# A four-layer sequence kernel: the convolution reads its input time-major from a second host layout, and the length mask moves to the dense stage

## What is computed

```python
# L0: per channel a causal convolution with a kernel of 1024 steps, masked by each sample's length
mask = arange(1024) < length[:, None]
u = x * mask[:, None, :]
x = x + (irfft(rfft(u, 2048) * rfft(kernel, 2048))[..., :1024] + u * D[:, None]) * mask[:, None, :]
# L1: per sample one of 16 channel mixes
x = x + einsum('bct,bcd->bdt', x, weights[condition])
# L2: dense 1024 x 1024 over time, bias, and one of 32 rank-16 adapters per sample
x = x + x @ W2.T + bias + (x @ A2[adapter].T) @ B2[adapter].T
# L3: dense 1024 x 1024, and one of 5 rank-32 adapters per sample
x = x + x @ W3.T + 0.5 * (x @ A3[labeler]) @ B3.T
```

## Time and profile before

| | us |
|---|---|
| median of 3 runs | 1579.5 (1578.61 to 1580.14) |
| span of the profiled execution | 1580.4 |
| convolution, 205.9 to 641.3 | 435.4 |
| dense stage from its first product, 663.6 to the end | 916.8 |
| TensorE busy | 1529.8 (97% of the span) |
| VectorE busy | 1002.2 (63%) |
| ScalarE busy | 612.5 (39%) |
| GpSimd busy | 389.7 (25%) |

### The profile page before, as it was taken

The page is one execution under the profiler, slowest core; times in us unless marked ns, Lnnn a source line. Parts: engine busy times, 40 slices in busy tenths (PEclk is TensorE's granted clock), DMA queues, the critical chain, the costliest instruction groups (busy, mean ns, idle before and its releaser), DMA issues.

```text
span 1580.4 us, 33596 instructions
## 1 busy us (share of the span) xinstructions
PE 1529.8 (97%) x11213; PEld 1477.5 (93%) x11213; DVE 1002.2 (63%) x2010; ACT 612.5 (39%) x1185; POOL 389.7 (25%) x389
## 2 busy tenths in 40 slices
PE   6899989999999999699999999999999999999998
PEld 5778879999999999599999999999999999999998
DVE  7955357888888888445556555565564555655554
ACT  3331245555555554234334343343343433434332
POOL 3551246666666666100000000000000000000000
PEclk9999999999999999699999999999999999999999
DMA  9723166666666674433533535435344353353542
GB/s 243 111 104 98 41 217 236 240 236 238 237 235 238 237 246 165 141 109 99 166 113 117 150 106 145 134 102 158 113 138 141 94 164 115 116 153 104 147 132 74
DMA packets 165111, 243.13 MB, mean 154 GB/s; under 512 B 62113, under 2 KB 118701, under 8 KB 162417
## 3 DMA queue, kind: packets, MB, share of 16 engines
q1 hardware_dynamic: 154844, 208.11, 43.7%
q10 hardware_dynamic: 10230, 34.52, 6.1%
HBM read 167.62 MB, written 74.95 MB: 153 GB/s over the span
## 4 chain that ended last, share of the span: by engine, by line
PE 58%; issue 0%; ACT 0%; DVE 0%; DMA 0%; DVEq 0%
PE ps L1538 23%; PE ps L1539 22%; PE ps L1509 7%; PE ps L1548 2%; PE ps L1546 2%; PE ps L1520 1%; PE ps L1515 0%; DMA x_in<-x_d 0%; ACT a L1310 0%; DVE weights L1406 0%; ACT xa L1312 0%; ACT weights L1322 0%; DVE y_out L1487 0%; ACT xs L1327 0%; DVE y_out L1490 0%
## 5 line engine op out<-in xcount | busy, mean ns | idle before, releaser
L1538 PE MATMUL ps<-weights,xs 128*128 128x256 f32 x1536 | 398.4, 289 | 0.0
L1539 PE MATMUL ps<-weights,xs 128*128 128x256 f32 (+1 forms) x1536 | 389.9, 293 | 0.0
L1538 PE MATMUL ps<-weights,xa 128*128 128x352 f32 (+1 forms) x1152 | 331.1, 314 | 4.4 <-DVE weights L1406 1.3
L1539 PE MATMUL ps<-weights,xa 128*128 128x256 f32 (+1 forms) x1152 | 325.9, 298 | 0.0
L1538 PEld LDWEIGHTS ps<-weights,xs 128*128 128x128 f32 x1536 | 293.2, 191 | 0.0
L1539 PEld LDWEIGHTS ps<-weights,xs 128*128 128x128 f32 x1536 | 292.4, 190 | 0.0
L1284 POOL COPY m_gath<-mix 64x64 f32 x128 | 37.6, 294 | 840.8 <-PE ps L1509 733.9
L1110 PE MATMUL ps<-toep,ut 128*128 128x512 f32 (+2 forms) x1152 | 228.8, 344 | 0.0
L1538 PEld LDWEIGHTS ps<-weights,xa 128*128 128x128 f32 x1152 | 219.1, 190 | 9.7 <-issue 9.7
L1539 PEld LDWEIGHTS ps<-weights,xa 128*128 128x128 f32 x1152 | 218.9, 190 | 0.0
L1310 ACT ACTIVATE a<-ps 128x512 f32<-128x512 f32 x128 | 76.6, 598 | 358.1 <-PE ps L1509 358.1
(11 more groups left out here) (227 smaller groups left out, 2483.5 us busy)
## 6 DMA issues: line engine op xcount, KB each, us to landing
toep_raw<-kern_d SPq DMA_DIRECT2D x64, 512.0 KB, 3.4
xt<-in_x SPq DMA_DIRECT2D x64, 512.0 KB, 4.0
x_d<-xt SPq DMA_DIRECT2D x64, 512.0 KB, 2.9
x_in<-x_d SPq DMA_DIRECT2D x64, 512.0 KB, 5.0
out<-y_out ACTq DMA_DIRECT2D x64, 512.0 KB, 4.4
stack<-b_d SPq DMA_DIRECT2D x130, 128.0 KB, 3.4
tab<-a_d SPq DMA_DIRECT2D x126, 128.0 KB, 2.1
stack<-b_d SPq DMA_DIRECT2D x128, 64.0 KB, 4.2
```

The lines of the kernel that those rows point to most:

```text
L1538: mm(left[0], x_part, left[1], start=first and is_wide, stop=end, skip_group_check=True)
L1539: ins = mm(right[0], x_part, right[1], start=first and is_wide and H_AT[m] > 0, stop=end, skip_group_check=True)
```

## The change

- The host hands over a second copy of x, `in_xt`, with axes (channel, step within a block of 128, block, sample). The convolution loads its operand from it, steps on the partitions (`xt[u][p, block, sample]`, 512 KB, four buffers, up to 3 ahead). `transpose_x` and `utf` go; `ut`, `udiff` and the diagonal product read `xt` itself.
- The sums of lags are made once for all channels in the preamble, on the kernel as it lies in DRAM: load `fold_in` (64 x 1024), one addition on VectorE, store `fold_d`. A channel's tile comes in two DMAs, 768 columns of `kern_d` and 640 of `fold_d`. `fold` and `toep_low` on GpSimd go; VectorE makes the whole low part of the tile, 1408 columns.
- The mask goes from the convolution. What it stores to `x1_d` is the unmasked result, through four buffers `yo`: ScalarE copies the shared quarter and the first half (`front`), after a new semaphore `half_done` that TensorE gives in the middle of the channel; VectorE adds and subtracts for the second half (`back`). SP's `store_y` waits for both.
- In the dense stage x is loaded beside x1 (`x_nat`, 512 KB a tile), two pairs ahead, and VectorE chooses (`choose`): a comparison of the step number (int16, 256 columns, a quarter at a time) with the samples' lengths, then a predicated copy of x over x1 where the step is too late. Each pair has four such choices of 512 columns for the next pair; a quarter of the mixing now waits for `chosen`. The first pair's four are made at the start of the stage.
- SP: per channel one more DMA, the tile loads now ahead of the x load and the store; in the dense stage two waits and two loads between `load_c` and the wait for `p_done`. TensorE's last group of channels stays inside its loop. GpSimd's addition to `mix` has no channel loop ahead of it any more.

```diff
-    mask, o_x = at("mask", [P, T], U8, o_mask)
+    lens_cols, o = at("lens_cols", [P, TILES], F32, o_mask)
+    ramp, o = at("ramp", [P, QT], I16, o)
+    o_x = o_mask + T
+    assert o <= o_x
...
+    toep_view = bass.AP(tensor=kern_d.tensor, offset=QT, ap=[[T + P, C], [1, P], [1, TOEP]])
+    fold_view = bass.AP(tensor=fold_d.tensor, offset=0, ap=[[FW, C], [1, P], [1, TFOLD]])
...
+            sp.wait_ge(kern_stored, 32)
+            sp.dma_start(fold_in[:], kern_d[:, 0:T]).then_inc(in_fold, 16)
             sp.wait_ge(job_free, freed("la3"))
             sp.dma_start(a2_d.rearrange("a p n -> p a n"), lora2_out[:].rearrange("p a c r -> p a (c r)")).then_inc(a2_stored, 16)
+            sp.wait_ge(fold_ready, 1)
+            sp.dma_start(fold_d, fold_sum[:]).then_inc(fold_stored, 16)
...
             def load_x(k, u):
-                if not isinstance(k, int) or k > 0:
-                    sp.wait_ge(x1_stored[u], 16 * k)
-                elif u in (6, 7):
-                    sp.wait_ge(b2_stored, 16 * (AR // P))
-                sp.dma_start(xt[u][:], x[:, bass.ds(UNROLL * k + u, 1), :].squeeze(1)).then_inc(x_in[u], 16)
+                ready(sp, conv_done, UNROLL * k + u - BUFS + 1)
+                sp.dma_start(xt[u % BUFS][:], xt_in[bass.ds(UNROLL * k + u, 1)].squeeze(0)).then_inc(x_in[u % BUFS], 16)
             def load_toep(k, u):
                 h = UNROLL * k + u
                 ready(sp, toep_hi, h - 1)
                 ready(sp, toep_lo, h - 1)
-                ready(sp, dt_lo, h - 1)
-                sp.dma_start(toep_raw[u % 2][:, RAW0:], toep_view[bass.ds(h, 1), :, :].squeeze(0)).then_inc(toep_in[u % 2], 16)
-            def store_x1(k, u):
-                sp.wait_ge(x1_ready, UNROLL * k + u + 1)
-                sp.dma_start(x1_d[:, bass.ds(UNROLL * k + u, 1), :].squeeze(1), xt[u][:]).then_inc(x1_stored[u], 16)
-            sp.wait_ge(kern_stored, 32)
+                raw, landed = toep_raw[u % 2], toep_in[u % 2]
+                sp.dma_start(raw[:, TFOLD:], toep_view[bass.ds(h, 1), :, :].squeeze(0)).then_inc(landed, 16)
+                sp.dma_start(raw[:, 0:TFOLD], fold_view[bass.ds(h, 1), :, :].squeeze(0)).then_inc(landed, 16)
+            def store_y(k, u):
+                sp.wait_ge(y_front, UNROLL * k + u + 1)
+                sp.wait_ge(y_back, UNROLL * k + u + 1)
+                sp.dma_start(x1_d[:, bass.ds(UNROLL * k + u, 1), :].squeeze(1), yo[u % BUFS][:]).then_inc(x1_stored[u % BUFS], 16)
+            sp.wait_ge(fold_stored, 16)
...
+                if loads or u < UNROLL - 2:
+                    load_toep(k + (u + 2) // UNROLL, (u + 2) % UNROLL)
                 if loads or u < UNROLL - AHEAD:
                     load_x(k + (u + AHEAD) // UNROLL, (u + AHEAD) % UNROLL)
-                if loads or u < UNROLL - 3:
-                    load_toep(k + (u + 3) // UNROLL, (u + 3) % UNROLL)
-                store_x1(k, u)
+                store_y(k, u)
...
-            def toep_low(k, u):
-                h = UNROLL * k + u
-                pool.wait_ge(toep_hi, h + 1)
-                nc.gpsimd.tensor_tensor(toep[u % 2][:, 1, 0:T], toep_raw[u % 2][:, :RAW0 - 1:-1], f(toep[u % 2][:, 0, 0:T]),
...
-            def fold(k, u):
-                k, u = k + u // UNROLL, u % UNROLL
-                pool.wait_ge(toep_in[u % 2], 8 * UNROLL * k + 16 * (u // 2) + 16)
-                raw = toep_raw[u % 2]
-                tt(raw[:, 0:RAW0], raw[:, RAW0:2 * RAW0], raw[:, RAW0 + QT:2 * RAW0 + QT], ALU.add).then_inc(fold_begun, 1)
-                pool.wait_ge(fold_begun, UNROLL * k + u + 1)
...
             def split_high(k, u):
                 h = UNROLL * k + u
-                act.wait_ge(folded, h + 1)
+                act.wait_ge(x_in[u % BUFS], x_count(k, u) + 16)
                 ready(act, conv_done, h - 1)
-                nc.scalar.activation(tri[u % 2][:], toep_raw[u % 2][:, :TOEP + TFOLD - P - 1:-1], ACT.Copy).then_inc(tri_ready, 1)
-                nc.scalar.activation(toep[u % 2][:, 0], toep_raw[u % 2][:, ::-1], ACT.Copy).then_inc(toep_hi, 1)
-                act.wait_ge(ut_ps, h + 1)
-                xp = ps[0].rearrange("p (i b) -> p i b", i=K8)
-                nc.scalar.activation(utf[u % 2][:, 0:2], xp[:, 2:4], ACT.Copy)
-                nc.scalar.activation(ut[u % 2][:, 0], xp, ACT.Copy).then_inc(ut_hi, 1)
-                nc.scalar.activation(utf[u % 2][:, 2], xp[:, K8 - 1], ACT.Copy).then_inc(utf_ready, 1)
+                copy(ut[u % 2][:, 0], xt[u % BUFS][:], ACT.Copy).then_inc(ut_hi, 1)
+                act.wait_ge(toep_in[u % 2], toep_count(k, u) + 32)
+                copy(toep[u % 2][:, 0], toep_raw[u % 2][:, ::-1], ACT.Copy).then_inc(toep_hi, 1)
+                copy(tri[u % 2][:], toep_raw[u % 2][:, :TOEP + TFOLD - P - 1:-1], ACT.Copy).then_inc(tri_ready, 1)
                 act.wait_ge(diff_ready, h + 1)
-                nc.scalar.activation(dt[u % 2][:, 0], udiff[:], ACT.Copy).then_inc(dt_hi, 1)
+                copy(dt[u % 2][:, 0], udiff[:], ACT.Copy).then_inc(dt_hi, 1)
+            def front(k, u):
+                h = UNROLL * k + u
+                act.wait_ge(half_done, h + 1)
+                ready(act, y_back, h)
+                copy(shared_in[:], ps[1][:, (u % 2) * HB:(u % 2) * HB + QT], ACT.Copy).then_inc(shared_out, 1)
+                ready(act, x1_stored[u % BUFS], x_count(k, u))
+                if isinstance(k, int) and k == 0 and u in (2, 3):
+                    act.wait_ge(b2_stored, 16 * (AR // P))
+                copy(yo[u % BUFS][:, 0:HB], ps[2 + u % 2][:, 0:HB], ACT.Copy).then_inc(y_front, 1)
+            def channel(k, u, ahead=True):
+                if ahead:
+                    split_high(k + (u + 1) // UNROLL, (u + 1) % UNROLL)
+                front(k, u)
...
+            dve.wait_ge(in_fold, 16)
+            tt(fold_sum[:], fold_in[:, 0:FW], fold_in[:, QT:QT + FW], ALU.add).then_inc(fold_ready, 1)
...
-            def transposed_low(k, u):
+            def split_low(k, u):
                 h = UNROLL * k + u
-                dve.wait_ge(utf_ready, h + 1)
-                tt(ut[u % 2][:, 1], ps[0].rearrange("p (i b) -> p i b", i=K8), f(ut[u % 2][:, 0]),
-                   ALU.subtract).then_inc(ut_lo, 1)
+                dve.wait_ge(x_in[u % BUFS], x_count(k, u) + 16)
+                ready(dve, dt_lo, h)
+                raw = xt[u % BUFS]
+                tt(udiff[:], raw[:, 0:2], raw[:, 2:4], ALU.subtract).then_inc(diff_ready, 1)
+                dve.wait_ge(ut_hi, h + 1)
+                tt(ut[u % 2][:, 1], raw[:], f(ut[u % 2][:, 0]), ALU.subtract).then_inc(ut_lo, 1)
                 dve.wait_ge(toep_hi, h + 1)
-                tt(toep[u % 2][:, 1, T:], toep_raw[u % 2][:, RAW0 - 1::-1], f(toep[u % 2][:, 0, T:]), ALU.subtract)
-                ready(dve, dt_lo, h)
-                tt(udiff[:], ps[0][:, 0:QT].rearrange("p (i b) -> p i b", i=2), utf[u % 2][:, 0:2], ALU.subtract).then_inc(diff_ready, 1)
+                tt(toep[u % 2][:, 1], toep_raw[u % 2][:, ::-1], f(toep[u % 2][:, 0]), ALU.subtract).then_inc(toep_lo, 1)
                 dve.wait_ge(dt_hi, h + 1)
                 tt(dt[u % 2][:, 1], udiff[:], f(dt[u % 2][:, 0]), ALU.subtract).then_inc(dt_lo, 1)
-            def masked(k, u):
+            def back(k, u):
                 h = UNROLL * k + u
-                y, shared = ps[2 + u % 2], ps[1][:, (u % 2) * HB:(u % 2) * HB + QT]
+                y, to = ps[2 + u % 2], yo[u % BUFS]
                 dve.wait_ge(conv_done, h + 1)
-                ready(dve, unfold_done, h)
-                nc.vector.tensor_copy(shared_in[:], shared).then_inc(shared_out, 1)
-                dve.wait_ge(chain, mask_made)
-                nc.vector.copy_predicated(xt[u][:, 0:HB], mask[:, 0:HB], y[:, 0:HB])
-                dve.wait_ge(shared_out, h + 1)
-                tt(y[:, HB:HB + QT], y[:, HB:HB + QT], shared_in[:], ALU.add)
-                tt(y[:, HB + QT:T], y[:, HB + QT:T], shared_in[:], ALU.subtract).then_inc(unfold_done, 1)
-                dve.wait_ge(unfold_done, h + 1)
-                dve.sem_inc(mask_begun, 1)
-                nc.vector.copy_predicated(xt[u][:, HB:T], mask[:, HB:T], y[:, HB:T]).then_inc(x1_ready, 1)
+                dve.wait_ge(y_front, h + 1)
+                tt(to[:, HB:HB + QT], y[:, HB:HB + QT], shared_in[:], ALU.add)
+                tt(to[:, HB + QT:T], y[:, HB + QT:T], shared_in[:], ALU.subtract).then_inc(y_back, 1)
...
-            def transpose_x(k, u):
-                h = UNROLL * k + u
-                pe.wait_ge(x_in[u], 16 * k + 16)
-                ready(pe, ut_lo, h)
-                ready(pe, diff_ready, h)
-                for i in range(K8):
-                    ins = nc.tensor.transpose(ps[0][:, i * P:(i + 1) * P], xt[u][:, i * P:(i + 1) * P], ident[:])
-                ins.then_inc(ut_ps, 1)
...
-                pe.wait_ge(tri_ready, h + 1)
-                ready(pe, x1_ready, h - 1)
+                ready(pe, y_front, h - 1)
...
+                pe.wait_ge(ut_lo, h + 1)
```

(39 more changed lines are left out.)

150 lines of the change are left out of this document (70 added, 80 removed).

## The result

The changed kernel takes 1583.2 us (median of 7 runs, 1578.0 to 1586.5) against 1578.6 of the kernel before in the same comparison: ratio 1.0025, interval 1.0013 to 1.0037. The forecast was 1560, and 1583 lies within its range, but the sign is wrong: it is slower by a little, about as much as the 0.2% named above. Its profiled execution has a span of 1581.1 us and a time of 1583.27.

What follows compares the result with a forecast made beforehand. TensorE's own work was taken to bound both stages. The span summed as 1580.4 - 54.2 - 1.0 - 6.2 - 4.6 - 1.8 + 2.8 + 45 = 1560.4 us, forecast as 1560, range 1530 to 1593.

Steps and rivals of the forecast that it cites:

- the convolution's channel at 5.76 us: Convolution: without transpositions a channel takes TensorE's 5.76 us of products, for 6.62, if the other engines keep up.
- The "third": Convolution: above 6.4 us from a tile's issue to landing, each further microsecond costs a third of one per channel.
- the tile loads bound the channel: Rival, convolution: at 8 us from issue to landing TensorE waits 0.5 a channel, +32 us, 1592; 12%.
- signs of being wrong named ahead: Whole kernel: h_rows starting as M2 ends, a channel over 6 us, or a dense-stage clock below 1.00.
- The start: Convolution's start: first group of transpositions goes, -1.0 us; less standing and half-speed clock, net -6.2 us.
- The end of the convolution: Convolution's end: TensorE's stand and half-speed clock go, -4.6 us; shorter finish -1.8, start of dense stage +2.8.
- The transpositions: Convolution: 63 groups of transpositions of 0.86 us leave TensorE, -54.2 us.
- VectorE's wide low part: Convolution: the tile's low part of 1408 columns takes VectorE 1.6 us, or 4.9 at the crowded price.
- The choices: Dense stage: two choices before h_rows, 2.9 us together, make TensorE stand 1.45 us a pair, +45 us (34 to 62).
- the rival in which it falls in each pair: Rival, dense stage: TensorE's stands drop its clock to 1.2 GHz in each pair, 53 us, 1613; 10%.
- Sheds less: Rival, convolution: VectorE or ScalarE keep 6.2 us a channel, while the pairs lose as summed, 1588; 5%.
- the first rival: Rival, dense stage: the choices are in time, 0 to 12 of the 45 us stay, 1515 to 1530; 13%.

Runs made afterwards that it cites:

- e9_conv_order: The changed kernel with SyncE's order per channel h: tile of h+3, x of h+4, then store of y(h); 1564.0 us, 0.9901 of the kernel before.
- e6_mix_later: The changed kernel with GpSimd's addition of the identity to mix held back until eight channels are done; 1586.7 us, 1.0052 of the kernel before.
- e7_rows_first_x_early: The changed kernel with h_rows(n,0) ahead of all choices and choice (n+1,0,1) right after y11's addition; 1536.9 us, 0.9734 of the kernel before.
- e3_rows_first: The changed kernel with h_rows(n,0) ahead of the choices and choice (n+1,0,1) behind the sums; 1636.7 us, 1.0361 of the kernel before.

## Why the prediction was wrong, step by step

**The step that failed: the convolution's channel at 5.76 us**, "the tile's way from load to load ... above 6.4 us from issue to landing each further microsecond costs a third". The form of the step was right: SyncE's bunch, the tile behind y's store, ScalarE's turn for it. Its sizes were not. I had the landing 6.2 to 7.1 us after the channel's start, before ScalarE's 7.2. It came at 8.6 in the channel shown (400.02 against 391.40): its second part was issued at 2.5 and took 6.2 to land. Two causes show in the rows. The transfer beside others moved 286 to 292 GB/s at a share of 0.91, not the 363 at 0.99 of the earlier trace rows, a stretch at the convolution's start. And the two parts were issued at 2.0 and 2.5, where I had begun to count at 1.2 to 3 for the whole bunch, with y's 512 KB 0.7 us ahead. The "third" was too mild also. From the first part's issue to the second's landing are 6.7 us, so that rule gives 0.1 a channel, while 0.32 to 0.35 was lost. It followed the tile's buffer from load to load and left out y's store, by which the way is shorter. In the channel shown, the load sets out behind the store at the start of channel h, and its tile is wanted at the start of channel h + 2:

```profile
401.44 1.62 DVE L929 TENSOR_TENSOR toep<-toep_raw,toep 128x1408 fp32r<-128x1408 f32 x1 [1.65 <-ACT toep L646]
...
402.98 0.42 DVE L931 TENSOR_TENSOR dt<-udiff,dt 128x256 fp32r<-128x256 f32 x1
...
403.63 0.77 PEld L1088 LDWEIGHTS ps<-toep,dt 128*128 128x128 f32 x6 [0.27 <-issue]
```

From 391.40 to 403.63 are 12.23 us for two channels, 6.12 each, where 2 x 5.76 = 11.52 would do: issue at 2.0, landing at 8.6, high part to 10.0, low parts to 12.0, first product at 12.2. On this way each microsecond costs half of one, and a late issue costs as much as a long landing. From the third channel (221.15) to the last (592.10) 61 steps took 370.95 us: 61 x (6.08 - 5.76) = 19.6 us of the missing 23. e9_conv_order, whose tile loads no longer stand behind that store, gives 19.2 back. Why the tile's transfers run slower than the earlier trace rows was not tried.

The rival "the tile loads bound the channel" held this mechanism, at 0.5 us a channel and 12%, and its 1592 is nearer than my 1560. It was priced by issue to landing alone. What it lacked is that an order of the queue could take it away, which only the runs show.

Two of the signs of being wrong named ahead came true: the mean channel is over 6, and the dense stage's clock is below 1.00 (see below).

**The start**, -1.0 and -6.2: too large by 2.9 us. The first product came at 207.7 for 204.9, the third channel at 221.15 for 218.2. I had moved GpSimd's addition to mix from the convolution's end to its front and counted the gain at the end, but not the VectorE work beside which it then lies. TensorE stood 2.68 us for VectorE there, and behind that the granted clock was 0.55 until 211.0, which I had not counted either; the second tile's landing, at 210.2 for my 209, was then no longer waited for. Without the addition (e6_mix_later) that tile lands at 211.3 and is waited for, and the third channel comes at 223.0: one of the two alone was enough for the delay.

**The end of the convolution**: right. With no GpSimd work there, the last channel runs 6.0 us at full clock, and TensorE's stand has gone. From the last product to the first mixing product are 10.35 us for 9.54, +0.8 for my +1.0 (-1.8 and +2.8).

**The transpositions**, -54.2: right as work. With the loads in time a step is 5.75, so TensorE sheds 0.87 a channel.

**VectorE's wide low part**: 1.625 us for 1.6 at mean over 64, not the crowded 4.9. It has two inputs in SBUF and GpSimd idle beside it, as the rule of the Trainium skill's page "SBUF — State Buffer" quoted ahead would have it.

**The choices**, +45: right in mechanism and size, +42.7. A mask instruction took 345 ns (0.35 in the sum), a choice with its copy 1.40 and 1.38 for 1.5 and 1.4. x1 came 4.8 us after issue for 4.5. The stage gives 46.3 back with the choices behind h_rows (e7_rows_first_x_early).

**The clock**: the rival in which it falls in each pair priced that at 53 us. It fell in one pair. TensorE stood 0.5 to 2.1 us before the transposition of hrow in 30 of the 32 pairs; behind the longest of these stands the clock was 0.50, 1.2 GHz, for 3.4 us, behind the others it stayed at 1.00:

```profile
1233.77 0.33 PE L1531 MATMUL ps<-ident,hrow 128*128 128x128 f32 x1 [2.05 <-DVE hrow L1444]
1234.64:1238.05 3.41, 3.41 (x17) 3.41 (x16) 2.47 (x9) 0.00 (x0) 0.00 (x0) 0.50 0.34 98
```

That pair took 32.2 us for 29.9. The rest of the stage's 0.99 stands at its start (0.50 from 620 to 625 us) and its end. So the rival was wrong in how often, not in kind: e3_rows_first, with longer stands, had ten such falls. The margin was small: in the change stands of up to 1.71 us kept the clock, and in e3_rows_first one of 1.82 us lost it.

"Sheds less", by VectorE or ScalarE, did not happen: both waited for a DMA, not for work.

**A rival's bound**: 0 to 12 of the 45 us kept give 1515 to 1527, not 1530, so by its own terms the first rival lay wholly outside the range. Nothing measured hangs on it.

Put together: 1560.4 predicted, +19.6 in the steps, +2.9 at the start, -2.3 in the pairs, and the small rest, make the 1581.1 measured.

## What to carry to other kernels

When a change takes compute out of a loop, lay the DMA queue's issue order out for the shorter loop, each issue at the time when its own condition is met and each behind the waits that stand ahead of it. A load behind a store's wait is late by the whole wait, and a faster loop makes that visible. Moving one of them alone can be worse than none, since whatever follows inherits its wait.

Before a new job goes in front of an old one on an in-order engine, ask which of the two someone waits for. Then ask what the job's end releases: a choice made 6 us later let 1 MB of loads set out just ahead of the output's stores and cost 3.3 us a pair (dense stage 1016.2 in e3_rows_first for 913.2 in e7_rows_first_x_early).
